# Recurrence stage of a four-layer kernel: broadcast two steps ahead into three PSUM banks, the pieces beside it in three banks in place of four

## What is computed

```python
xa = _ln(x, ln1_w, ln1_b)
sx = jnp.concatenate([state[:, 1:2] - xa[:, :1], xa[:, :-1] - xa[:, 1:]], axis=1)
xxx = jnp.tanh((xa + sx * maa_x) @ maa_w1) ...          # five mixing vectors
xk, xw, xv, xr, xg = ...                                # xa + sx * (stack + xxx)
w = jnp.exp(-jnp.exp(time_decay + jnp.tanh(xw @ td_w1) @ td_w2))
r, k, v, g = xr @ Wr.T, xk @ Wk.T, xv @ Wv.T, silu(xg @ Wg.T)
def step(s, rkvw):
    a = k_t[..., :, None] * v_t[..., None, :]
    out = jnp.einsum('bhi,bhij->bhj', r_t, u * a + s)
    s = a + w_t[..., :, None] * s
# then a group norm of out, the gate, Wo, and the gated mixing layer
```

## Time and profile before

| what | value |
|---|---|
| median of 3 runs | 1978.76 us (1978.57 to 1981.2) |
| the profiled execution's own time | 1977.81 us |
| its span in the trace | 1975.7 us |
| granted PE clock, mean over the span | 0.974 |
| PE busy | 1875.9 us (95%) |
| DVE, ACT, POOL busy | 1113.9, 1044.2, 996.6 us |
| recurrence, first to last step | 397.65 to 636.1 us |

### The profile page before, as it was taken

One profiled execution on the slowest core, in us unless ns is written; L12 is line 12 of the kernel. 1 busy time (PEld: TensorE's weight loads), 2 busy tenths in 40 slices (PEclk: granted clock), 3 DMA queues, 4 the chain that ended last, 5 costly groups with the idle time before them and its releaser, 6 DMA issues.

```text
span 1975.7 us, 39304 instructions
## 1 busy us (share of the span) xinstructions
PE 1875.9 (95%) x15088; PEld 1551.0 (79%) x15088; DVE 1113.9 (56%) x2104; ACT 1044.2 (53%) x1945; POOL 996.6 (50%) x1140
## 2 busy tenths in 40 slices
PE   7999999988897899999999999999999998999999
PEld 5777779534454788899999999999999987977788
DVE  4566656389989654444454444454444455755654
ACT  3565543434343656665665656556566554345532
POOL 6777731366654543654544544545454434347630
PEclk9999999889998999999999999999999999999999
DMA  6000010000000222232232232232232210000000
GB/s 236 2 2 2 2 57 1 1 0 1 1 1 11 91 81 75 83 104 83 82 106 82 81 107 82 81 107 82 81 102 87 81 60 22 22 29 16 2 11 33
DMA packets 61847, 108.11 MB, mean 55 GB/s; under 512 B 7008, under 2 KB 42336, under 8 KB 60256
## 3 DMA queue, kind: packets, MB, share of 16 engines
q1 hardware_dynamic: 60784, 103.38, 16.7%
q10 hardware_dynamic: 880, 2.22, 0.3%
HBM read 103.47 MB, written 2.10 MB: 53 GB/s over the span
## 4 chain that ended last, share of the span: by engine, by line
PE 84%; DVE 7%; issue 4%; POOL 3%; ACT 2%; DMA 0%; DVEq 0%; SPq 0%; ACTq 0%; POOLq 0%
PE banks L862 18%; PE banks L891 9%; PE banks L934 9%; PE banks L627 7%; PE banks L644 7%; PE banks L466 7%; PE banks L923 6%; PE banks L904 4%; PE banks L475 3%; PE banks L548 2%; PE banks L523 2%; PE banks L505 2%; PE banks L534 2%; PE banks L912 1%; PE banks L460 1%
## 5 line engine op out<-in xcount | busy, mean ns | idle before, releaser
L1983 POOL TENSOR_TENSOR w_lo<-w2ring,w_hi 128x512 fp32r<-128x512 f32 x128 | 176.1, 1376 | 254.9 <-ACT w_hi L1128 254.9
L2067 POOL TENSOR_TENSOR wo_lo<-wo_ring,wo_hi 128x256 fp32r<-128x256 f32 x128 | 94.6, 739 | 254.6 <-ACT wo_hi L1337 254.6
L1808 DVE TENSOR_REDUCE nmax<-banks 128x4 f32<-128x260 f32 x128 | 54.3, 424 | 280.2 <-PE banks L904 280.2
L1794 DVE TENSOR_TENSOR v<-banks,dbv 128x512 f32<-128x512 f32 x128 | 88.5, 692 | 201.6 <-PE banks L891 200.7
L1337 ACT ACTIVATE wo_hi<-wo_ring 128x256 fp32r<-128x256 f32 x128 | 53.3, 417 | 197.6 <-PE banks L934 197.5
L934 PE MATMUL banks<-wo_hi,c_hi 128*128 128x256 f32 x512 | 145.5, 284 | 4.4 <-DVE c_lo L1801 4.4
L934 PE MATMUL banks<-wo_lo,c_hi 128*128 128x256 f32 x512 | 145.4, 284 | 0.0
L934 PE MATMUL banks<-wo_hi,c_lo 128*128 128x256 f32 x512 | 145.3, 284 | 0.0
L1324 ACT ACTIVATE k<-banks,cols 128x512 f32<-128x512 f32 x128 | 88.1, 688 | 79.4 <-PE banks L862 79.4
L923 PE MATMUL banks<-PT,v 128*128 128x128 f32 x1024 | 125.3, 276 | 3.4 <-issue 3.4
L923 PEld LDWEIGHTS banks<-PT,v 128*128 128x128 f32 x1024 | 120.3, 192 | 3.8 <-issue 3.8
(11 more groups left out here) (235 smaller groups left out, 5525.1 us busy)
## 6 DMA issues: line engine op xcount, KB each, us to landing
w2ring<-in_w SPq DMA_DIRECT2D x128, 384.0 KB, 4.1
b2ring<-in_b SPq DMA_DIRECT2D x128, 128.0 KB, 4.5
wo_ring<-in_wo SPq DMA_DIRECT2D x128, 128.0 KB, 4.3
mlp_w<-in_mlp SPq DMA_DIRECT2D x6, 1024.0 KB, 7.1
wl<-in_wres SPq DMA_DIRECT2D x1, 2688.0 KB, 9.0
X<-in_x_in SPq DMA_DIRECT2D x4, 512.0 KB, 11.1
wb<-in_wres SPq DMA_DIRECT2D x2, 1024.0 KB, 10.8
ctxT<-in_ctx_in SPq DMA_DIRECT2D x4, 512.0 KB, 19.8
```

The lines of the kernel that those rows point to most:

```text
L1794: V.tensor_tensor(v2[:, :, 2 * half:2 * half + 2, :].rearrange("p s i d -> p i s d"), held(("v2", p, half))[:, :].rearrange("p (i s d) -> ...
L1983: G.tensor_tensor(w2_lo[:, n % 2, :], w2ring[:, n % HR, 0:2 * KT * P], w2_hi[:, n % 2, :].bitcast(f32), ALU.subtract).then_inc(S["l2_wlo"], 1)
L2067: G.tensor_tensor(wo_lo[:, n % 2, :], wo_ring[:, n % WR, :], wo_hi[:, n % 2, :].bitcast(f32), ALU.subtract).then_inc(S["l2_wolo"], 1)
```

## The change

`vb(n)` and `first_state(n)` are issued two steps ahead in place of one, and take three banks in turn (`THREE`, banks 0 to 2). The pieces beside them have three banks (`MIDDLE`, 3 to 5) in place of four. At the end of a chunk the order differs: pass 14 issues none, and pass 15 issues two, since the first step of the next chunk needs v of that chunk. ACT's order follows PE's. DVE and POOL are unchanged.

```diff
+AHEAD = {14: (), 15: (1, 2)}
...
-        TWO, MIDDLE = (0, 1), (2, 3, 4, 5)
+        THREE, MIDDLE = (0, 1, 2), (3, 4, 5)
...
-                    b = take(pe, ("vb", n), "l1_state", n + 1, TWO)
+                    b = take(pe, ("vb", n), "l1_state", n + 1, THREE)
...
-                    vb(0)
+                    for n in range(2):
+                        vb(n)
                     for n in range(CHUNKS * NS):
                         c, j = divmod(n, NS)
-                        if n + 1 < CHUNKS * NS:
-                            vb(n + 1)
+                        for ahead in AHEAD.get(j, (2,)):
+                            if n + ahead < CHUNKS * NS:
+                                vb(n + ahead)
...
-                    first_state(0)
+                    for n in range(2):
+                        first_state(n)
                     for n in range(CHUNKS * NS):
                         c, j = divmod(n, NS)
-                        if n + 1 < CHUNKS * NS:
-                            first_state(n + 1)
+                        for ahead in AHEAD.get(j, (2,)):
+                            if n + ahead < CHUNKS * NS:
+                                first_state(n + ahead)
```

## The result

The changed kernel takes 1999.33 us (median of four runs, 1995.41 to 1999.65), the kernel before 1978.66 beside it: a ratio of 1.0098, with a 95% interval from 1.0082 to 1.0114. It is slower by some 21 us. The forecast, 1983 us in a range from 1973 to 1990, had the direction right and the size wrong by a factor of five.

The account below looks back on a forecast made before the run. It took PE and DVE to bound the recurrence by turns. Waits less stalls, 0.3 + 2.8 + 2.7 - 2.9 = +2.9 us, plus 1.2 for the clock, made 4.1; carried to the median 1978.76, 1983 us, range 1973 to 1990.

Parts of the forecast that it names:

- the look-ahead: Starting states and broadcasts two steps ahead: DVE's stalls before its steps go, at most 14.4 us won by itself.
- the 8 that I had named: Sign to check: DVE's idle time before line 1653 falls from 18.4 to under 8 us, the rest being the entry.
- the four waits: Chunk 1, alike in chunk 2: second halves of z, pass 10 mix, v and pass 12 mix start late; chunk 1 2.8 us longer.
- 0.3 + 2.8 + 2.7 = 5.8 us: Time added: 0.3 ahead of the steps and in chunk 0 together, 2.8 in chunk 1, 2.7 in chunk 2.
- This marker: Sign to check: DVE's idle time before line 1604, waiting for hT, grows above 2.4 us in chunks 1 and 2.
- the clock, 1.2 us: New PE gaps in dense chunks 1 and 2 bring more time at half rate: 1.2 us added for both together.
- the sign of being wrong that I had named: The prediction is wrong if the low stretches of PE's clock change by more than a few us.
- Rival 4: Much slower: each 2.5 us gap brings a long 1.2 GHz stretch in two chunks, +7 on 2.9, some 1989 us; chance 0.14.
- my 2.9: Net slowdown in us over all chunks and ahead of the steps, before the clock was added.
- -2.9: Chunk 3: stalls of 5.2 us go, 2.3 come back through the late second half of the first mixing_in; 2.9 us gained.
- I had 0.3 for this stretch and chunk 0 together: Ahead of the steps and chunk 0: late exponential and PE delay, partly offset by an old v_lo wait; 0.3 us together.
- I had this part as unchanged: From the last step to the end of the kernel: the time stays the same.

## Why the prediction was wrong

**Right: the look-ahead.** DVE's stalls fell to 5.4 us, under the 8 that I had named. What that is worth in time is shown for the narrow ring alone, 12.4 us, and for chunk 3 with the waits out of its way, where it is nothing. With four banks beside it no run can show it, since the eight are all in use.

**Right in place, roughly in size: the four waits.** The second z half waited 2.31 us in chunk 2, where I had 2.5; in chunk 1 only 0.67, because z itself ran at half rate and filled the time. The pass 10 wait was 1.23 for 1.7, the pass 12 wait 0.3 for about 1. DVE stood 1.9 us for `tokens_first` in chunk 1, where I had 1.8. That agreement is luck: it stands behind the short wait of 0.67, and behind the full one, in chunk 2, DVE stood 3.5.

**Under-sized: what the waits pass on.** I had 0.3 + 2.8 + 2.7 = 5.8 us for the part ahead of the steps and chunks 0 to 2. At about the clock of the kernel before (18 us at half rate for its 21, in the run with the fronts first) chunks 0, 1 and 2 take 52.1, 63.2 and 64.5 us for 50.1, 59.4 and 61.1: 2.0, 3.8 and 3.4, 9.2 us in all. Ahead of the steps come 1.5 (below), so 10.7 against my 5.8. Two places were mis-sized. For `tokens_first` I had DVE begin its step 0.8 us late (2.2 on top of 464.70 is 466.9 and not the 466.5 of the text, so 1.2 by its own rows); it stood 3.5 us, against a stall of 0.9 before, in both chunks of that run. And in chunk 0, for which I had next to nothing, it stands anew for `mix`, 4.8 us there and 6.5 in the changed kernel's profile. I let DVE's loss be made good until hT, and forecast that the idle time in front of line 1604 grows above 2.4 us each time. In sum it fell, from 4.7 to 4.2 us: 1.4 at the start of chunk 1, 2.8 at the start of chunk 2, for 2.4 both times. DVE had lost its time earlier, at `gn_sum`, at r and at `gn`, and came to hT late itself. This marker failed at one of its two places.

**The step that failed: the clock, 1.2 us.** I took the low stretches of one chunk of the kernel before as the measure of what new gaps would bring, and added 1.8 at most for each of two chunks. The changed kernel spends 41 us of chunks 0 to 2 at the lower level of 1.2 GHz, the kernel before 21, so the sign of being wrong that I had named, a change by more than a few us, is there. The pair of runs with one order gives it a price: 8.2 us in chunks 0 to 2, and ahead of the steps 1.7 more (below): 9.9, eight times the term. It also feeds on itself, as PE and DVE in chunk 1 of the changed kernel show:

```profile
495.81 1.75 PE L715 MATMUL banks<-zB,wl 32*128 32x512 f32 x2 [1.23 <-ACT dtmp L1178]
...
498.51 5.82 PE L468 MATMUL banks<-xm,wl 128*128 128x512 f32 x8
```

```profile
506.30 1.29 DVE L1700 TENSOR_TENSOR aT<-banks,gateT 128x512 f32<-128x512 f32 x2 [3.94 <-ACT banks L1222]
```

Behind the wait the v projection takes 5.82 us in place of 3.67, so `gn` comes late, so DVE stands 3.94 us. In the run with the fronts first, with the same 1.23 us gap, PE's clock did not fall there:

```profile
496.49 1.12 PE L715 MATMUL banks<-zB,wl 32*128 32x512 f32 x2 [1.23 <-ACT dtmp L1178]
...
498.11 1.88 PE L468 MATMUL banks<-xm,wl 128*128 128x512 f32 x4
500.36 1.98 PE L468 MATMUL banks<-xm,wl 128*128 128x512 f32 x4 [0.38 <-DVE xm L1638]
```

Rival 4 named this mechanism, with 0.14. Its price of 7 us was not far off, though it had two long stretches where many short ones came; but it kept my 2.9 for all the rest, and so it stopped at 1989. The Trainium skill describes a case that I didn't weigh ("TensorE: Matmul & The Clock Gate", A second HAM failure mode: psum-queue depth-cycling): bf16 matmuls that cycle through PSUM banks with small idle times between the groups make the clock go back and forth, and the cost lies in the falls and rises. The trace agrees that the clock goes back and forth (41 us at the lower level for 21); here the cost shows in the matmuls themselves, 5.82 us for 3.67. The page gives no size for a case like this.

**Missing: the fronts of pass 12 in chunk 3.** I followed the 33 takes of a chunk with pieces and took chunk 3 from them, with one late wait. Its own pieces make a second: the second front waits for the gated product 3.62 us, `mixing_out` comes behind it, and DVE stands 4.50. Taking it away is worth 3.6 and 4.0 us in two pairs and some 3 in the third at a like clock. So -2.9 became +0.9 in the profile that is taken apart here. In the second profile of the same kernel it is -1.9 (63.9 for 65.8), so 2.8 us of this term go with the clock. And the -2.9 itself was too much: with the fronts out of the way and the clock alike the look-ahead gives 1.1 us in this chunk.

**Ahead of the steps.** The entry is only 1.4 us later, which hides more than it shows. The stretch from the `dec` matmuls (378.69, and 380.49 in the kernel before, in the views of the filled gaps) to the scan of step 0 takes 17.9 us in all six profiles with four banks there, 21.1 in all ten with three, and 19.4 in the one with the filled gap. So the narrow ring costs 3.2 us here, 1.5 for the wait and 1.7 for the slow v projection (5.37 for 3.67). I had 0.3 for this stretch and chunk 0 together. The changed kernel's profile came to that stretch 1.8 us earlier, by code that the change leaves alone.

**Behind step 63.** I had this part as unchanged, and it is 1.6 us longer. That is not the change's: the five other profiles with the rings of the kernel before (three of them with the new rings in chunk 3) have 1342.7 to 1343.9 there, the changed kernel 1342.5 and 1342.6. It is the first profile, with 1340.9, that is short. Why is not known.

By these terms: 10.7 (waits, to the end of chunk 2) + 9.9 (clock, the same stretch) + 0.9 (chunk 3) - 1.8 + 1.6 (neither of the change) = 21.3 us. The forecast fell short by 4.9 in the waits, 8.7 in the clock and 3.8 in chunk 3; the clock is the largest, but putting it right alone would have given some 1992 us.

## What to carry to other kernels

When two rings share a fixed number of banks, price the bank that is taken by a run of its own or by walking every take, the rare pieces of the last chunk too; here the bank taken cost 33.6 us, and the bank given won back 12.4 of them. In a stage where PE is dense, a list of new waits is only half of the cost: compare PE's busy time for the same matmuls and the granted clock by stage, and take the clock as a term as large as the waits. And before a buffer is added against a stall, try to move the reader: the bonus two passes earlier gave 5.2 us with no bank at all, and no version with the deeper look-ahead beat the plain one with the same edits.

## What I had not expected of the hardware

- One order of instructions can have two patterns of low clock, 8.2 us apart over 180; the dear one was seen twice and repeated the lengths of chunks 0 to 2 within 0.1 us, the cheap one once. Chunk 3 of the same kernel differed by 2.8 us between its two profiles. A comparison of two kernels in a dense stage should look at the granted clock before it gives the difference to an edit.
- At one place a gap of 0.88 us was followed by half rate in ten of ten profiles and one of 0.97 in none of six. The 0.88 has two gaps of 0.20 beside it. The length of the longest gap alone does not tell.
- ACT's table load, 1.28 us, starts only when the instruction in front of it is through, so an unrelated copy that waits for PE delays the exponential by the load too. The Trainium skill ("ScalarE: Activation LUTs", What ACT_TABLE_LOAD costs) gives about 1283 ns for the load, which the trace confirms, and another 1380 for a drain, which it does not show: the load begins at 489.03, as soon as the copy of 488.82 ends, and the exponential starts at 490.32.
